# Who copies the transposed exponentials: half of those of the third and fourth query chunk go from ScalarE to VectorE

## The reference

```python
xn = layernorm(x over channels and pixels) * ln_g + ln_b
Q, K, V = 1x1 head projection + 3x3 depthwise conv of xn      # 8 heads of 24 channels
x = w_f applied to (V @ softmax(K^T Q / alpha)) + b_f + xn      # channel attention
t = tokens of x                                                 # 1024 tokens x 192
...
qkv = layernorm(t) @ W_qkv                                      # 6 heads of 32
wei = softmax(causal(q @ k^T * 32**-0.5))                       # 1024 x 1024 per head
out = ((wei @ v) @ W_proj + b_proj) @ W_proj + b_proj
t = t + out
t = t + mixture of 4 experts, the best 2 of them, on layernorm(t)
```

## Time and profile before

| | us |
|---|---|
| median of 3 runs | 3315.94 (3314.32 to 3317.31) |
| the profiled execution, its own time | 3319.14 |
| its span | 3317.3 |
| granted TensorE clock, mean | 0.986 |
| PE busy | 3075.1 (93%) |
| DVE busy | 2204.9 (66%) |
| ACT busy | 1871.7 (56%) |
| copies by ScalarE (L1557) | 768, 396.8 busy |
| copies by VectorE (L1107) | 384, 184.9 busy |

### The profile page before, as it was taken

How to read it: one execution, slowest core, us unless ns; L and a number is a source line. 1 busy time by engine, 2 the same in 40 slices (tenths; PEclk the granted TensorE clock), 3 DMA queues, 4 the chain that set the end, 5 groups by cost and what they waited for, 6 DMA issues and landing times.

```text
span 3317.3 us, 72524 instructions
## 1 busy us (share of the span) xinstructions
PE 3075.1 (93%) x26642; PEld 2349.3 (71%) x26642; DVE 2204.9 (66%) x5632; ACT 1871.7 (56%) x3996; POOL 875.3 (26%) x1142
## 2 busy tenths in 40 slices
PE   4999999999989999999999999988999999999995
PEld 1666667666666676666766666667888888888884
DVE  3777677677776777777767777664565655655653
ACT  0647466475474664745746547464555555555553
POOL 2121303313123032131330322352133233233223
PEclk9999999999999999999999999999999999999997
DMA  7547445454464554644545447334667767767673
GB/s 178 142 113 174 123 115 149 123 156 119 124 165 115 136 138 115 173 115 126 150 124 148 127 113 183 100 130 147 187 219 221 216 202 217 216 209 225 202 215 118
DMA packets 256517, 519.83 MB, mean 157 GB/s; under 512 B 70919, under 2 KB 161991, under 8 KB 246521
## 3 DMA queue, kind: packets, MB, share of 16 engines
q1 hardware_dynamic: 222878, 453.58, 48.7%
q0 software_dynamic: 29184, 59.81, 6.0%
q10 hardware_dynamic: 4107, 1.81, 0.3%
HBM read 242.82 MB, written 117.71 MB: 109 GB/s over the span
## 4 chain that ended last, share of the span: by engine, by line
PE 67%; DVE 14%; issue 10%; ACT 3%; POOL 2%; DMA 2%; SPq 1%; DVEq 0%; ACTq 0%; POOLq 0%
PE ps L2042 13%; PE ps L1855 9%; PE ps L2058 9%; PE ps L1720 5%; PE ps L1843 5%; PE ps L2063 5%; PE ps L1804 3%; PE ps L1877 3%; PE ps L1887 2%; PE ps L2018 2%; PE ps L1812 2%; ACT p_sb L1543 2%; DVE minus_max L1094 1%; PE ps L1895 1%; PE ps L2027 1%
## 5 line engine op out<-in xcount | busy, mean ns | idle before, releaser
L1094 DVE TENSOR_REDUCE minus_max<-ps 128x1 f32<-128x128 f32 (+7 forms) x768 | 571.7, 750 | 246.9 <-PE ps L1845 231.3
L1543 ACT ACTIVATE p_sb<-ps,minus_max 128x128 f32<-128x128 f32 (+7 forms) x768 | 569.3, 741 | 41.0 <-DVE minus_max L1094 37.0
L1855 PE MATMUL ps<-ident,p_sb 128*128 128x128 f32 x3456 | 532.1, 279 | 44.5 <-ACT p_sb L1543 19.1
L1665 ACT ACTIVATE g<-ps,bcur 128x512 f32<-128x512 f32 x402 | 276.8, 688 | 447.4 <-PE ps L2042 441.4
L1428 DVE TENSOR_TENSOR g_lo<-g,g_hi 128x512 fp32r<-128x512 f32 x402 | 282.2, 702 | 361.4 <-ACT g_hi L1666 361.4
L1557 ACT ACTIVATE PT<-ps 128x512 f32<-128x512 f32 (+3 forms) x768 | 396.8, 517 | 134.4 <-PE ps L1855 125.3
L1855 PEld LDWEIGHTS ps<-ident,p_sb 128*128 128x128 f32 x3456 | 371.8, 142 | 99.4 <-ACT p_sb L1543 38.4
L2058 PE MATMUL ps<-w_all,g_hi 128*128 x1608 | 437.1, 352 | 1.6 <-DVE y_rows L1452 1.6
L1843 PE MATMUL ps<-KS,QS 96*128 96x512 f32 (+3 forms) x1152 | 393.6, 401 | 21.2 <-ACT p_sb L1543 19.6
L1720 PE MATMUL ps<-ring,wconv 125*32 125x512 f32 (+1 forms) x3072 | 357.1, 605 | 16.6 <-DMA ring<-padded_scratch 16.6
L817 POOL DMA_INDIRECT routed_rows<-xhat,slot x256 | 253.8, 991 | 345.6 <-issue 345.6
(11 more groups left out here) (293 smaller groups left out, 5462.7 us busy)
## 6 DMA issues: line engine op xcount, KB each, us to landing
ring<-padded_scratch SPq DMA_DIRECT2D x576, 204.0 KB
cur<-w_all SPq DMA_DIRECT2D x65, 1536.0 KB, 7.1
routed_rows<-zero_rows SPq DMA_DIRECT2D x67, 384.0 KB, 5.1
xgt<-routed_rows SPq DMA_DIRECT2D x67, 384.0 KB, 4.5
expert_rows<-y_rows SPq DMA_DIRECT2D x67, 384.0 KB, 3.1
padded_scratch<-xpad SPq DMA_DIRECT2D x32, 435.0 KB, 3.6
x_sb<-x SPq DMA_DIRECT2D x16, 768.0 KB, 5.4
KS<-QKh SPq DMA_DIRECT2D x128, 96.0 KB
```

Source lines behind the costliest of these rows:

```text
L1094: v.tensor_reduce(nmx[:, qc, h:h + 1], score_place(n), AX, ALU.max, negate=True).then_inc(mx_sb, 1)
L1543: a.activation(p_sb[n % NP][:, 0:P * (qc + 1)], score_place(n), ACT.Exp, bias=nmx[:, qc, h:h + 1], accum_out=ls[:, qc, h:h + 1]).then_inc( ...
L1665: a.activation(g32[:, n % 2, :], bank(n % 2), ACT.Gelu, bias=b1)
L1855: last = t.transpose(bank(pass_bank(piece))[:, P * k:P * (k + 1)], p_sb[n % NP][:, P * (k0 + k):P * (k0 + k + 1)], ident[:, :])
```

## The change

In the third and fourth chunk (`qc` 2 and 3) the pieces of heads 1, 3 and 5 are copied by VectorE, those of heads 0, 2 and 4 still by ScalarE. VectorE's first such copy of an image gets the wait for the key and query loads that ScalarE's copy of unit 12 also has, since `PT[1]` lies where these loads read.

```diff
+        SHARED_COPIES = (2, 3)
...
-                        eng = "dve" if k0 else "act"
+                        eng = "dve" if k0 or (qc in SHARED_COPIES and h % 2) else "act"
...
+                        if n == 2 * H + 1:
+                            stacks_loaded(dve, i, 1)
                         if n == H * TPC:
                             stacks_loaded(dve, i, 2)
```

## The result

The change makes the kernel a little slower: 3325.85 us median of 7 runs (3323.94 to 3330.74), beside 3315.94 us (3311.24 to 3319.58) for the kernel before. The ratio is 1.003, with a 95% interval of 1.002 to 1.004. The forecast was 3328 us, with 3315 to 3338 as its range. The changed kernel's profiled execution has a span of 3322.2 us.

What follows compares the result with a forecast made beforehand. No engine paces the whole; the chain of waits between engines decides. 0.55 + 0.2 + 0.05 = 0.8 us per image, times 15 = +12 us: profiled 3319.14 becomes 3331, less 3.2 to the median gives 3328 us, range 3315 to 3338.

Steps and rivals of the forecast that it cites:

- Sign and size: Whole kernel: slower by 0.8 us per image, +12 us over 15 images.
- Unit 13 and 15, `deviation` 0.83 late: Third chunk: both copies on VectorE make `deviation` 0.83 us late, so unit 16's blocks start 0.55 us late.
- Units 17 and 19 free: Third and fourth chunk: these copies fall where VectorE waited or sat idle; cost 0.
- Unit 21, 0.2 us: Around `gain`: the copy behind it makes unit 24's `score_max` 0.76 us late, 0.2 us more on the path.
- Unit 23, 0.05 us: Fifth chunk: the copy behind unit 25's `score_max` makes unit 26's 1.35 us late; 0.05 us taken, between 0 and 1.35.
- The sixth chunk 0.2 shorter: Seventh image's attention: the sixth chunk becomes about 0.2 us shorter than before.
- The last image: Without image steps ScalarE paces its third and fourth chunk, up to 0.6 us each; worth 0 through a fifth-chunk weight load.
- The rival of a pacing VectorE: VectorE paces all of the fifth chunk, unit 26's 1.35 us stay: 20 us slower, 3336 us; chance 0.18.
- The faster rival: ScalarE paces the third and fourth chunk, so its relief gains 14 us, 3302 us; chance 0.12.

Runs made afterwards that it cites:

- undoing the order: The changed kernel with `deviation` placed in front of unit 15's copy on VectorE: 3316.54 us beside 3314.58 for the kernel before, ratio 1.0005.
- unit 13 alone: The kernel before with only unit 13's copy moved to VectorE: one execution, 3326.47 us beside 3317.24; third chunk 7.30 us (+0.13).
- e8: The kernel before, `variance` in front of unit 21's `score_max` and the row sums' reciprocal in front of each head 0's `score_max`: 3291.38 us, ratio 0.9928.
- Unit 23 alone: The kernel before with only unit 23's copy moved to VectorE: one execution, 3313.26 us beside 3315.34; chunk lengths together 0.09 us longer.
- e3: The kernel before with only the copies of units 17 and 19 moved to VectorE: 3314.65 us beside 3314.58, ratio 1.0005.
- e7: The kernel before with the next image's `variance` moved in front of unit 21's `score_max` on VectorE: 3308.20 us beside 3315.34, ratio 0.9977.
- the kernel with the third chunk only: The kernel before with only the copies of units 13, 15 and 17 moved to VectorE: 3323.32 us beside 3314.58, ratio 1.0024.

## Why the prediction was right, point by point

- *Sign and size.* The expected 0.8 us per image was 0.88 in chunk lengths: 13 us over 15 images. The medians differ by 9.9 us. The profiled spans differ by 4.9 us only: in that execution of the changed kernel the images' periods exceed their median by 6.9 us less (last section), and the fifth chunk of its last image is 1.9 us shorter.
- *Unit 13 and 15, `deviation` 0.83 late.* `deviation` begins 5.97 us after unit 12's exponentials, 0.83 later than 5.14, and unit 16's blocks wait for it. Cost 0.59 in place of 0.55, since the slack was 0.23 us and not 0.28. Shown by undoing the order and by unit 13 alone. ScalarE's idle time in front of the norms grew by 0.37 us, not by 0.5.
- *Units 17 and 19 free.* Shown: 0.
- *Unit 21, 0.2 us.* Measured alone 0.22. Here the step was exact.
- *Unit 23, 0.05 us.* Measured alone 0.09; units 21 and 23 together cost 0.29 to 0.30 us in the full change, not 0.25. This term had been chosen between 0 and 1.35 us by the nearest row, not worked out, so that it came so close is partly luck. The prediction had left out the wait for the bank of the piece before (`passed`): in the full change unit 24's second piece waits for unit 23's copy at 956.67. With unit 23's copy alone that wait is taken up, and the 0.09 us arise at the end of the chunk.
- *The sixth chunk 0.2 shorter.* It was 0.04 shorter. I had taken the last 0.2 us of VectorE's lateness (1.0 to 0.8) as given back there; most of it was given back inside the fifth, where `score_max` is 1.31 us late at unit 26 and 0.92 us at unit 29.
- *The last image.* This step failed. I read "ScalarE busy 6.15 of 6.32 us" as ScalarE pacing, and expected up to 0.6 us from each chunk. With its copies gone the chunks last as long to the hundredth, ScalarE busy 5.39 and 6.08 us:

```profile
2155.10:2161.42 6.32, 6.05 (x62) 4.39 (x60) 5.28 (x14) 5.39 (x18) 0.52 (x2) 1.00 1.00 215
2161.42:2168.85 7.43, 7.03 (x80) 5.44 (x78) 6.24 (x14) 6.08 (x18) 0.53 (x2) 1.00 0.96 364
```

  ScalarE is busy 1.94 us less in the two chunks, and that became waiting: in front of the norms it sat idle 0.9 us, where before no such wait is listed, and for transposes 2.0 us instead of 0.8. TensorE is the fullest engine there now, busy 6.05 of 6.32 and 7.03 of 7.43 us. That ScalarE did not pace shows in e8 as well, where the third chunk of the last image took 6.15 us with all copies on ScalarE. The step cost the total nothing, since the prediction had set the last image's worth at 0 for another reason, the weight load in its fifth chunk, which no run tested: that chunk lasted 16.07 us before and 14.18 us after, and 11.3 to 18.1 us in the experiments, so that its sign (longer by what the others lose) can't be read. The Trainium skill's advice, to use ScalarE and VectorE both for the evacuation of PSUM (TensorEngine Tiling (Array Packing), PSUM Bottleneck), is given there for the case that the evacuation may have become the bottleneck. Here it had not, and no trace agrees with the shortening that the prediction drew from it: even in the last image, where VectorE had time, the split gained nothing.
- *The rival of a pacing VectorE.* In the fifth chunk VectorE is busy all the time, but the delay at unit 26, forecast as 1.35 us and measured as 1.31, did not stay: 0.88 us were left in the sixth chunk. Unit 23 alone shows it too.
- *The faster rival.* Refuted by e3, e7 and the last image.

## What to carry to other kernels

A busy share near one does not say that an engine paces: ask which of its instructions another engine waits for, and what follows it in its own list. Work moved to another engine costs by its place in that engine's order: in front of a result that is awaited it costs nearly its whole length, less what slack is left, in an idle gap nothing, and the same move in another order can be free. Where a chain through several engines starts at a short operation, try doing that operation one place earlier before moving any long one: here 0.7% against the change's loss of 0.3%.

## What the runs showed of the hardware that I had not expected

TensorE pauses for 1 to 3 us now and then, at no semaphore that the profile shows, and it does so at the same places. In the seventh image such a pause stands in the `two_heads` multiplications of the eighth chunk, before the change 2.90 us, after it 0.98 us, and in 13 of the 14 profiled executions at least 0.98 us, always 64 to 67 us after the image's first exponentials. In the tenth image it stands in the `two_heads` of the seventh chunk, before the change and after it:

```profile
1384.66 0.41 PE L1887 MATMUL ps<-PT,v_sb 128*32 128x128 f32 x4 [1.75 <-issue]
```

```profile
1387.92 0.41 PE L1890 MATMUL ps<-PT,v_sb 128*32 128x128 f32 x4 [2.19 <-issue]
```

There the seventh chunk took 14.09 and 15.67 us instead of 11.94. The second image has one in 4 of the 14 executions, the tenth in 5, the twelfth in one, and no other image any of 0.75 us or more in its attention. So these pauses keep their places, and what varies from execution to execution is how long they are, up to none at all. Apart from them the second chunk is 1.2 to 2.5 us longer in one to three images of 7 executions, in changing images; I did not look into that. What they are stays open, and no run was made for it. One thing that the traces show may be a lead: in each of the five pauses that were looked into (three before the change, one after it, one in the kernel with the third chunk only), the profile's instruction queue records a single packet in 8 to 12 us, and the matmuls go on 2.7 to 3.0 us after it. That TensorE waits for its own instructions there is a guess from this.

Of the profiled executions, the images' periods exceed their median by 16.1 us in total before and by 9.2 us after. Not all of it is pauses: the last of these periods, between the fifteenth and the sixteenth image, is 3.0 to 5.7 us longer in every execution, outside the causal attention. The difference of 6.9 us is still half of the effect that was to be measured, so a single execution of each kernel is not enough to size it.
